# Two graph transformer layers on one core: two stages in another order, and all four blocks closed without GpSimd's drain

## The reference

```python
deg = jnp.maximum(segment_sum(ones, dst, 1250), 1.0)
xn = layernorm(x)
x = x + gnn0(xn, src, dst, deg, ...) + mix0(xn)      # mix0: flow attention and a two-layer network with gelu
x = x + ffn0(layernorm(x))                           # one expert of 16 for the whole graph, chosen by the mean row
xn = layernorm(x)
x = x + gnn1(xn, src, dst, edge_weight, ...) + mix1(xn)   # normalised convolution, flow attention
x = x + ffn1(layernorm(x))                           # each node: the two best of 8 experts, gated, 512 -> 2048 -> 512

# gnn0: mean of the neighbours' rows @ W_neigh + row @ W_self + bias, then layernorm
# flow attention, 8 heads of 64:
q, k, v = sigmoid(x @ Wq + bq), sigmoid(x @ Wk + bk), x @ Wv + bv
sink, source = 1 / (q . k.sum(nodes)), 1 / (k . q.sum(nodes))
c_sink, c_source = q . (k * source).sum(nodes), clip(k . (q * sink).sum(nodes), -1, 1)
out = (q * sink) @ (k^T @ (v * softmax(c_source) * n)) * sigmoid(c_sink) @ Wo + bo
# gnn1: dinv = rsqrt(weighted in-degree); (A h)[dst] += h[src] * dinv[src] * w * dinv[dst]; @ W_lin + b_lin
# ffn0: scores = softmax(mean(x) @ Wg + bg); e = argmax; out = scores[e] * (x @ We[e] + be[e])
```

## Time and profile before

| | us |
|---|---|
| median of three runs (1926.17 to 1927.8) | 1926.62 |
| the profiled execution | 1927.84 |
| its span, from the first to the last instruction | 1926.0 |
| TensorE busy in the span | 1701.5 |
| VectorE busy | 895.7 |
| GpSimd busy | 751.2 |
| ScalarE busy | 542.1 |

### The profile page before, as it was taken

How to read it: one execution, slowest core, us unless ns; L and a number is a source line. 1 busy time by engine, 2 the same in 40 slices (tenths; PEclk the granted TensorE clock), 3 DMA queues, 4 the chain that set the end, 5 groups by cost and what they waited for, 6 DMA issues and landing times. The chain is left out here.

```text
span 1926.0 us, 26185 instructions
## 1 busy us (share of the span) xinstructions
PE 1701.5 (88%) x8051; PEld 1108.9 (58%) x8052; DVE 895.7 (47%) x2244; ACT 542.1 (28%) x1504; POOL 751.2 (39%) x866
## 2 busy tenths in 40 slices
PE   5589988987588888898699997799999999999998
PEld 4134434545477777544344455677677677677675
DVE  7932277345699999788566567100000000000002
ACT  0011101122488888401111134121121122122113
POOL 0577777777788888740111100400000000034005
PEclk9999989999799999999799998899999999999999
DMA  8000092000300000202200042756304400520003
GB/s 250 2 2 2 9 361 59 13 23 13 80 1 0 1 0 0 55 1 85 69 1 0 1 175 116 222 196 240 141 22 191 191 22 16 196 70 16 22 16 118
DMA packets 76225, 144.19 MB, mean 75 GB/s; under 512 B 21809, under 2 KB 23425, under 8 KB 71941
## 3 DMA queue, kind: packets, MB, share of 16 engines
q1 hardware_dynamic: 49415, 118.60, 17.4%
q0 software_dynamic: 18976, 10.95, 2.5%
q10 hardware_dynamic: 7776, 13.97, 2.2%
HBM read 107.75 MB, written 35.69 MB: 74 GB/s over the span
## 5 line engine op out<-in xcount | busy, mean ns | idle before, releaser
L338 POOL DMA_INDIRECT sorted_edges<-fa_records,fa_edge_slot x313 | 312.6, 999 | 155.3 <-issue 100.4
L2058 PEld LDWEIGHTS et_ps_h<-ex_turned,arena 128*128 128x128 f32 x3072 | 348.1, 193 | 21.5 <-issue 21.5
L2058 PE MATMUL et_ps_h<-ex_turned,arena 128*128 128x128 f32 x3072 | 348.4, 276 | 10.3 <-issue 10.3
L2068 PE MATMUL et_ps_y<-arena,et_hidden_t 128*128 x768 | 337.5, 592 | 0.0
L1968 DVE TENSOR_SCALAR ex_turned<-et_ps_t,ex_ln_g,ex_ln_b 128x128 f32<-128x128 f32 x96 | 32.8, 404 | 584.1 <-PE et_ps_t L2038 584.1
L2068 PEld LDWEIGHTS et_ps_y<-arena,et_hidden_t 128*128 128x128 f32 x768 | 142.2, 190 | 160.7 <-issue 160.7
L1054 POOL TENSOR_SCALAR ad_row<-iota,ad_edges 128x128 fp32r<-128x128 f32 x295 | 211.3, 728 | 40.3 <-PE ad_ps L1130 30.7
L1107 ACT ACTIVATE ad_row_high<-ad_row,ad_edges 128x128 fp32r<-128x128 f32 x472 | 184.2, 391 | 50.0 <-DVE ad_row L1076 34.7
L1129 PE MATMUL ad_ps<-ad_to,ad_row_high 128*128 128x320 f32 x472 | 153.0, 336 | 51.2 <-ACT ad_row_high L1107 48.2
L1939 POOL DMA_INDIRECT xn_rows<-slot_out,from_slots x10 | 12.2, 1217 | 475.6 <-POOLq L1936 472.8
L1074 DVE TENSOR_SCALAR ad_to<-iota,ad_edges 128x320 fp32r<-128x320 f32 x472 | 169.7, 419 | 9.8 <-DMA ad_edges<-sorted_edges 9.8
(11 more groups left out here) (399 smaller groups left out, 2155.0 us busy)
## 6 DMA issues: line engine op xcount, KB each, us to landing
arena<-L_ffn_W SPq DMA_DIRECT2D x16, 4096.0 KB, 18.4
slot_rows<-fa_zeros SPq DMA_DIRECT2D x1, 7424.0 KB, 28.0
slot_out<-fa_zeros SPq DMA_DIRECT2D x1, 7168.0 KB, 50.0
slot_out<-et_y ACTq DMA_DIRECT2D x24, 256.0 KB, 2.0
et_rows_in<-slot_rows ACTq DMA_DIRECT2D x24, 256.0 KB, 2.7
sorted_edges<-fa_records,fa_edge_slot POOLq DMA_INDIRECT x313
arena<-x SPq DMA_DIRECT2D x1, 2240.0 KB
neighbour<-fa_Wv SPq DMA_DIRECT2D x10, 224.0 KB
```

The source lines that it names most:

```text
L338: nc.gpsimd.indirect_dma_start(g.sorted_edges, bass.IndirectOffsetOnAxis(ap=self.edge_slot[0:rows, e:e + 1], axis=0), self.records[0:rows, ...
L2058: last = pe.matmul(ps_h[:, f % 2, i, :], x.weights[:, at:at + P], turned[:, k, :], start=(k == 0), stop=(k == KD - 1))
L2068: last = pe.matmul(ps_y[:], hidden_t[:, i, :], x.weights[:, bass.ds(buffer * (2 * HALF) + (HALF + i * D), D)], start=(i == 0), stop=(i == ...
```

## The change

It has three parts.

1. All four blocks are made with `no_gpsimd_drain=True`. At the end the four other engines drain as before; GpSimd goes to the barrier without a drain.
2. Block 1. The sums of q and k: VectorE adds the tiles up (`add_to_sums`, 18 additions of 125 x 512), and TensorE multiplies the two totals by ones once. VectorE prepares two tiles ahead, before the biases of the tile. `attend` uses ps_b and ps_c in turn, so TensorE waits for the tile before last. The second layer's rows are prepared three ahead. ScalarE clears the seven parts that GpSimd cleared, in pieces (`clear`), one in each step of the attend and of the second layer's loop; VectorE clears three tiles' width before its last addition and work2's part after it.
3. Block 3. The sum for the in-degrees is made in two parts, tiles 0 and 1 (FIRST_T = 2) behind product 0, tiles 2 to 4 behind product 1. A_LAG is 5. The weighted degrees come behind product 9. `inverse_root`, temperature and `conv_spread` stand before the wait for the gate. b_lin, bo and w_lin are loaded first, on a semaphore of their own. The wait for the other weights moves, on TensorE, to the first projection, and on VectorE behind the bias row. TensorE's bias row waits for the choice (`shifted_ready`).

The diff without the lines that only name semaphores:

```diff
...
-        block = stack.enter_context(nc.Block())
+        block = stack.enter_context(nc.Block(no_gpsimd_drain=True))
...
-            pool.wait_ge(s["d_out"], T + 1)
-            for part in (qkv[:, 0], qkv[:, 1, 2:], wo, mixed_w, kv_t, k_sum, q_sum):
-                nc.gpsimd.memset(part, 0.0).then_inc(s["cleared"], 1)
...
+            def add_to_sums(t):
+
+                for name, of, total in (("q", q, q_sum), ("k", k, k_sum)):
+                    dve.wait_ge(s[name + "_ready"], t + 1)
+                    if t > 1:
+                        dve.wait_ge(s[name + "_summed"], t - 1)
+                    v.tensor_tensor(total[r, :], tile(of, 0) if t == 1 else total[r, :], tile(of, t),
+                                    ALU.add).then_inc(s[name + "_summed"], 1)
...
-            staggered(c, 4, prepare, add_biases, nothing)
+            prepare(0, 0)
+            prepare(1, 1)
+            for t in range(T):
+                if t + 2 < T:
+                    prepare(t + 2, t % 2)
+                if t >= 2:
+                    add_to_sums(t - 1)
+                add_bias("q", ps_a, q, t)
+                add_bias("k", ps_b, k, t)
+                if t == T - 1:
+                    add_to_sums(t)
+                add_bias("v", ps_c, v_, t)
...
+            for t in range(3):
+                prepare_ff(t, t % 2)
+            for t in range(T):
+                if t + 3 < T:
+                    prepare_ff(t + 3, (t + 1) % 2)
...
+            def clear(part):
+                n = part.shape[1] // D
+                nc.scalar.copy(part.rearrange("p (n d) -> p n d", n=n),
+                               positions.zeros[:].unsqueeze(1).broadcast_to([P, n, D])).then_inc(s["act_cleared"], 1)
...
+                if t < len(behind_mix):
+                    clear(behind_mix[t])
...
+                if t < len(behind_attend):
+                    clear(behind_attend[t])
...
-            def add_sums(t, u):
-                pe.wait_ge(s["q_ready"], t + 1)
-                pe.matmul(ps_q, ones, tile(q, t), start=is_tile(t, 0), stop=is_tile(t, T - 1))
...
+            pe.wait_ge(s["q_summed"], T - 1)
+            pe.matmul(ps_q, ones, q_sum[0:NT, :], start=True, stop=True)
+            pe.wait_ge(s["k_summed"], T - 1)
+            pe.matmul(ps_k, ones, k_sum[0:NT, :], start=True, stop=True).then_inc(s["sums_done"], 1)
...
-                pe.wait_ge(s["d_out"], t + 1)
-                linear(ps_b, u, mixed_w).then_inc(s["d_done"], 1)
+                if t >= 2:
+                    pe.wait_ge(s["d_out"], t)
+                linear((ps_b, ps_c)[u], u, mixed_w).then_inc(s["d_done"], 1)
...
-A_LAG = 4
+A_LAG = 5
+FIRST_T = 2
...
+            for buffer, name in ((b_lin, "gnn_b_lin"), (bo, "mix_bo")):
+                load_row(sp, buffer, A["L1_" + name], s["lin_in"])
+            sp.dma_start(w_lin, A["L1_gnn_W_lin"]).then_inc(s["lin_in"], 16)
...
-            v.reduce_sum(in_sum[r, 0, 0:MID], counts[r, :, 0:MID].rearrange("p b n -> p n b"), AX_X).then_inc(s["summed"], 1)
+            for n in (slice(0, FIRST_T * NT), slice(FIRST_T * NT, MID)):
+                v.reduce_sum(in_sum[r, 0, n], counts[r, :, n].rearrange("p b n -> p n b"), AX_X).then_inc(s["summed"], 1)
...
+            inverse_root()
+            dve.sem_inc(s["roots_ready"], 1)
+            dve.wait_ge(s["tail_in"], 16 * 5)
+            c.link(v.reciprocal(temperature[:], temperature[:]))
+            v.tensor_scalar(conv_spread, g.ones[:], b_conv[:, 0:1], None, ALU.mult).then_inc(s["spread_ready"], 1)
...
+            dve.wait_ge(s["lin_in"], 16 * 3)
+            c.link(v.tensor_tensor(b_lin, b_lin, bo, ALU.add))
...
+            dve.wait_ge(s["qkv_in"], 16 * 7)
...
+                if t == 0:
+                    pe.wait_ge(s["summed"], 1)
+                    degrees(0, 6, range(FIRST_T), s["degrees"])
...
-                if t == 8:
+                if t == T - 1:
...
-            pe.wait_ge(s["qkv_in"], 16 * 10)
+            pe.wait_ge(s["lin_in"], 16 * 3)
             pe.wait_ge(s["spread_ready"], 1)
+            pe.wait_ge(s["shifted_ready"], 1)
...
+                    if not t and name == "q":
+                        pe.wait_ge(s["qkv_in"], 16 * 7)
...
```

More of the change, by code:

```diff
@@ L699, in attended @@
                 dve.wait_ge(s["d_done"], t + 3)
-                c.link(v.tensor_tensor(work2[r, u, :], out(ps_b), rows["bo"][r, :], ALU.add))
+                c.link(v.tensor_tensor(work2[r, u, :], out((ps_b, ps_c)[u]), rows["bo"][r, :], ALU.add))
                 v.tensor_tensor(tile(v_, t), work2[r, u, :], tile(g.xn, t), ALU.add).then_inc(s["d_out"], 1)
@@ L1311, in nodes @@
         banks = m.psum("banks", [P, 8, D])
-        names = ("own_in qkv_in rest_in tail_in half_summed weight_summed summed degrees weight_degrees product_done taken "
+        names = ("own_in lin_in qkv_in rest_in tail_in half_summed weight_summed summed degrees weight_degrees product_done taken "
                  "ec_ready ec_normed turned_out moved_out gate_done logits scored shifted_ready chosen fetched odds_ready gate_ready "
@@ L1514, in _ @@
             c.link(v.tensor_scalar(top0[:], top0[:], total[:, 0:1], None, ALU.mult))
-            dve.wait_ge(s["tail_in"], 16 * 5)
-            c.link(v.reciprocal(temperature[:], temperature[:]))
-            dve.wait_ge(s["qkv_in"], 16 * 10)
-            v.tensor_scalar(conv_spread, g.ones[:], b_conv[:, 0:1], None, ALU.mult).then_inc(s["spread_ready"], 1)
-            c.link(v.tensor_tensor(b_lin, b_lin, bo, ALU.add))
             dve.wait_ge(s["row_done"], 1)
@@ L1734, in _ @@
                 product(t)
+                if t == 0:
+                    pe.wait_ge(s["summed"], 1)
+                    degrees(0, 6, range(FIRST_T), s["degrees"])
                 if t == 1:
[L1736 to L1737 removed]
+                    pe.wait_ge(s["summed"], 2)
+                    degrees(0, 7, range(FIRST_T, HALF_T), s["degrees"])
                 if t == 2:
```

61 lines of the change are left out of this document (31 added, 30 removed).

## The result

| | before | changed |
|---|---|---|
| median of four runs on one chip, us | 1926.66 (1926.17 to 1927.8) | 1893.17 (1891.19 to 1895.17) |
| ratio to before | | 0.9825, 95% interval 0.9808 to 0.9842 |
| profiled execution, us | 1927.84 | 1891.19 |
| its span, us | 1926.0 | 1889.2 |

The median fell by 33.5 us, where 35.6 were forecast; the profiled execution of the changed kernel is its fastest of four and that of the kernel before its slowest, so the two profiles differ by more, 36.8 us of span.

What follows compares the result with a forecast made beforehand. Each block was taken to end with its last engine's drain, GpSimd's in blocks 1 and 3. Terms -17.5 (block 1), -13.7 (block 3 to expert row) and -4.4 (closing 3) gave -35.6, 1891.0 us; range 1887 to 1903.

Steps and rivals of the forecast that it cites:

- The bound: Block 4's expert tiles, 669 us with TensorE busy 668.46, keep their length; every microsecond won before them reaches the end.
- The drain: Closings of the blocks: 7.17 us of drain goes in block 1, 4.4 us in block 3, 0 in blocks 2 and 4.
- Block 1: Flow attention: -20.0 us for drain and moved memsets, +2.5 for slower stores; -17.5, between -20 and -14.
- the stream: Block 1, GpSimd's 313 indirect stores: becomes the bound; VectorE's additions cost 2.0 us, operations newly beside it 0.5.
- The rule of the full lock: Block 1: VectorE's 18 additions would block GpSimd's stores for their whole 0.69 us, 12.4 us instead of 2.0.
- TensorE's slack in block 1: Projections give 26 us, so TensorE's last work comes at 463, 10 us ahead of GpSimd's last store.
- Block 3 to the gate: Block 3's start to the gate's sum: combination 0 8.8 us earlier, 0.4 and 0.6 given back; -7.8, between -9 and -6.
- Gate to expert row: Block 3, gate's sum to first expert row: 10.6 us instead of 16.53; -5.9, between -3 and -6.1.
- (a): Rival, closings 1 and 3: the drain is not saved, only moved to GpSimd's next work; 1902.6 us, chance 0.08.
- (b): Rival, block 1: full lock on the ports, 18 additions block the stores for 12.4 us; 1901.4 us, chance 0.06.
- (c): Rival, expert tiles of block 4: slower, because TensorE's granted clock falls there; chance 0.03.
- (d): Rival, block 3: expert's row gains nothing, held to G + 16.5 by transfers or low clock; 1896.9 us, chance 0.12.

Runs made afterwards that it cites:

- two reversals: Changed kernel with GpSimd's drain back in all four blocks: 0.9899 of before; changed kernel with the seven memsets back on GpSimd: 0.9925 of before.

## Why the prediction was right, point by point

The mechanisms held, but the sum came out as near as it did partly by luck: its errors ran against each other. Block 1 gave 4.1 us more than forecast (21.6 for 17.5), block 3 up to the first store 2.2 less (11.5 for 13.7), its closing 0.9 less (3.5 for 4.4).

**The bound.** Right: block 4 kept its length to 0.7 us, and every microsecond won before it arrived. Blocks 2 and 4 did not notice their drains: GpSimd's ended at 793.8 and 1915.0 in the kernel before, the last engine's at 800.3 and 1923.8.

**The drain.** Right in kind at both places, and shown by putting it back: 7.2 us in closing 1, whole. In closing 3 the forecast took 4.4 us; the pair shows 3.5, all profiles 17.1 - 13.3 = 3.8. ScalarE's last group, which is next, began 11.9 us behind the first store instead of 11.2.

**Block 1.** The 20.0 us of the drain and the memsets are shown by two reversals (7.2 and 12.7). The step that failed in the profiled pair is the stream: 2.5 us were added for VectorE's 18 additions, and the last store came 1.4 us earlier instead (471.73 to 470.32; the stores' mean is 995 ns, where about 1005 was forecast). The stretched stores in it are 38 instead of 41, 11.5 us above normal instead of 11.9; the rest is the normal store, 0.958 us at the median instead of 0.962. Five of the 38 lie beside the additions, by up to 0.52 as in the earlier trace rows, 1.6 us together (0.6 to 2.7 in six profiles with the additions): the price of one was right, but the preparations no longer met the stores as often. Over all executions on the chips of the usual kind the old order started its last store at 469.3 to 471.7, the new one at 469.6 to 474.2, so that -1.4 and +2.5 are both in what one execution can show; the changed kernel with the old projections, which has no such additions, started it at 474.6. The rule of the full lock, named in the forecast from the Trainium skill, "SBUF — State Buffer", section "Who interferes with whom", would have made 12.4 us; for stores beside these additions no trace shows more than 0.52 of a pair's 1.38 us. One store at the end of the second layer was stretched by more. It runs beside VectorE's memset of 128 x 1536, which the change put there, and the last tile's additions, and took 1.73 us in the changed kernel, 0.77 over normal, and 2.03 in its repeat:

```profile
442.84 1.73 POOL L338 DMA_INDIRECT sorted_edges<-fa_records,fa_edge_slot  x1 [0.30 <-issue]
```

The 0.5 taken for operations that newly run beside the stream is of that size.

**TensorE's slack in block 1.** The projections gave 26 us: the changed order ends at 443.38, with the old projections at 469.10. Attend and second layer gave another 14 to 18 (to 469.10 from 486.74, or from 483.38 where no long memset holds VectorE up), for which the forecast had only "add to it"; its 10 us from TensorE's last work to GpSimd's memsets were 29.5 (442.8 to 472.36). The projections' share did not show in the time, as GpSimd is last. Of the three things done in block 1, the new order is worth 11 us, because without it TensorE's chain ends at 489.7, and the projections alone are worth nothing beside the other two edits.

**Block 3 to the gate.** 7.8 us were forecast, 7.3 came in the pair, and over all profiles 6.9 - 1.3 = 5.6. The start is set by the own rows, as forecast, 13.6 to 14.8 us behind the block's start instead of 12.8. That start is the mis-sized term: 8.8 us were forecast, 8.0 came in the pair and 6.9 over all, where the old order stands with a mean of 21.0 and the profile of before with 21.6. Behind combination 0 the forecast added 0.4 + 0.6. The 0.4 of the third pair of small operations is there in every profile. The overlap with GpSimd's sums, the 0.6, shows in VectorE's two additions of each combination: 21.6 and 21.3 us in the pair, 22.2 and 22.9 over all, so it was right over all and not in the pair. The sums end 43 us after the block's start either way, and the run without eight of them put the price of the whole overlap at 8.1 us. What had no term is TensorE's clock at the gate's last row: from the last combination to the gate's sum 9.1 us instead of 8.5 in the pair, 0.3 over all. In the changed kernel TensorE was idle for 7.43 us ahead of that row (6.35 before) and worked on it at the lower of its two levels throughout:

```profile
895.00:897.00 2.00, 2.00 (x11) 1.46 (x10) 1.14 (x6) 1.33 (x2) 0.00 (x0) 0.50 0.00 0
```

**Gate to expert row.** Right in mechanism (G is the gate's sum): in the pair be's transfer is the last arm, issued at G + 4.8 as before, and the row starts at G + 11.35 instead of 10.6, because the landing took 6.5 us instead of 5.7. The other arm, which was the uncertain one, was shorter than feared in this execution: TensorE made the row and the spreads in 1.10 and 2.39 us where the earlier trace rows have 2.04 and 4.46; its granted clock was 1.00 there:

```profile
899.00:901.00 2.00, 1.48 (x7) 0.81 (x7) 1.70 (x8) 0.46 (x3) 0.00 (x0) 1.00 0.00 0
```

The clock had been low just before, at the gate's last row, and rose to 1.00 at the gate's sum. Other executions had it otherwise. In four of the nine profiles of the new order it stayed at 0.50 for 8 us behind the gate's sum, with the row at 2.04 us and the spreads at 4.2 to 4.4, as in the earlier trace rows; there TensorE released the first expert row, at G + 11.85 to 11.99, which is the upper end that the forecast gave to that arm. In the five others be's transfer released it, at G + 10.65 to 11.35. Over all profiles the gain is 4.0 instead of 5.9, for this reason and since the profile of before, with 16.5 and 10.2 us of low clock behind the gate's sum (6.8 to 7.2 in the four others), is the longest of its order. A forecast from one execution took that length for the rule. Which of the edits of block 3 brought which part of this stretch no run separates.

**What had no term.** The late stretch of block 3 cost 1.0 in the pair and 0.7 over all. Together with the above it makes block 3 up to the first store 9.6 - 0.7 = 8.9 us shorter over all, 11.5 in the pair, 13.7 in the forecast. That can account for the 3 us by which the medians differ less than the profiles do.

**The rivals.** (a) fell by the run with the drains. (b) fell as said. (c) did not occur: the clock was 1.00 over the expert tiles. (d) in part: in the pair be's transfer took back 0.7 of its 5.9 us, and in four executions the low clock 1.3 to 1.4.

## What to carry to other kernels

Ask of each closing which engine is last and by how much: a drain is worth what it stands out beyond the next engine, and a cover that is taken away can lay open a delay that it hid (here 5 us in one VectorE instruction). When a queue of one engine sets a block, take work off the tail of that queue first; reordering the others pays only until they are under it. Here TensorE's last work was brought 29.5 us ahead of GpSimd's memsets, and the run with the old projections, where it is 5.6 us ahead, was no slower by its stages. Reading stages by milestones in several profiles showed effects of one to three microseconds that medians with a spread of ten could not.

## What the runs showed of the hardware that was not expected

- A GpSimd drain behind 313 indirect stores and some memsets took 7.165 us in each of four executions, though all stores had landed; one that began ahead of seven stores 17.0 to 17.3 us, ending 6.4 to 6.7 us after the last of them; one in a block without indirect stores 0.5 us.
- A VectorE tensor_scalar with one input in SBUF (L256, 125 x 512) took 0.54 us alone, and 2.07, 5.51 and 4.53 us beside GpSimd's memsets. Each time it ended 0.3 us after a memset did: twice that of 128 x 5120 (4.37 us long), in the case of 5.51 the next one, of 128 x 4096. The Trainium skill, "SBUF — State Buffer", section "Who interferes with whom", says that tensor_scalar can enter a mode in which it takes the ports that it shares with GpSimd, and then blocks or is blocked for a whole instruction: the traces agree, and show a wait over two instructions once.
- Block 2, whose code is the same in all kernels, took 300.1 to 301.8 us in five profiles and 303.4 to 304.3 in nine. Most of the difference (3.0 of 4.0 us in the two below) is one line of VectorE beside GpSimd's own tensor_scalar: means of 418 to 420 ns in the short ones, 424 or 425 in the long ones, 472 times. One of each:

```profile
L1074 DVE TENSOR_SCALAR ad_to<-iota,ad_edges 128x320 fp32r<-128x320 f32 x472 | 169.7, 419 | 9.8 <-DMA ad_edges<-sorted_edges 9.8
```

```profile
L1074 DVE TENSOR_SCALAR ad_to<-iota,ad_edges 128x320 fp32r<-128x320 f32 x472 | 172.7, 425 | 2.4 <-DMA ad_edges<-sorted_edges 2.4
```

  (kernel before; the same without the drain.) What sets an execution on the one or the other is open; the short ones come with the old order and with the new one.
- On one chip block 1 took some 300 us more in every kernel, with GpSimd's stores at their usual pace (977 to 984 ns in the mean) and the other three engines at rest again and again while they ran, VectorE for up to 43 us at a time. The cause is open; the new order gained more there, 26.5 us of block 1 instead of 11.
